# Attention of an adaLN layer: scores from two fp16 parts, the product with V in two halves of queries, and another order of the work around the maxima

## What is computed

```python
h = _layernorm(x, axis=-1) * (1 + ca) + sa
q = (hidden_states @ Wq).reshape(b, s, N_HEADS, HEAD_DIM)      # b, s = 1, 1024; 16 heads of 16
k = (hidden_states @ Wk).reshape(b, s, N_KV_HEADS, HEAD_DIM)   # 4 heads
v = (hidden_states @ Wv).reshape(b, s, N_KV_HEADS, HEAD_DIM)
q = _apply_rope(q, position_ids)
k = _apply_rope(k, position_ids)
scores = jnp.einsum('bshd,bthd->bhst', q, k) * scale
attn = jax.nn.softmax(scores, axis=-1)
out = jnp.einsum('bhst,bthd->bshd', attn, v)
return out.reshape(b, s, HIDDEN) @ Wo
```

## Time and profile before

| | before |
|---|---|
| median of 3 runs | 431.61 us (431.3 to 431.68) |
| the profiled execution, first to last instruction | 458.5 us |
| PE busy | 423.1 us, 92% |
| DVE busy | 318.8 us, 70% |
| ACT busy | 247.3 us, 54% |
| POOL busy | 152.9 us, 33% |
| granted TensorE clock, mean | 0.978 |

### The profile page before, as it was taken

How to read it: one execution, slowest core, us unless ns; L and a number is a source line. 1 busy time by engine, 2 the same in 40 slices (tenths; PEclk the granted TensorE clock), 3 DMA queues, 4 the chain that set the end, 5 groups by cost and what they waited for, 6 DMA issues and landing times.

```text
span 458.5 us, 9187 instructions
## 1 busy us (share of the span) xinstructions
PE 423.1 (92%) x3449; PEld 224.7 (49%) x3449; DVE 318.8 (70%) x739; ACT 247.3 (54%) x406; POOL 152.9 (33%) x177
## 2 busy tenths in 40 slices
PE   8999899999999999999999998987879878979995
PEld 4555323333333333333577776654545545646673
DVE  6878998999999999943476995464544343345457
ACT  1566678788878888887735254333123223233062
POOL 3068201220303030301210008565655764655400
PEclk9999999999999999999999999989979988999998
DMA  8500000000000000000110762488977886896192
GB/s 270 214 4 2 1 1 2 0 2 1 0 1 1 1 1 2 1 1 0 47 36 12 244 245 67 155 283 297 305 258 257 272 299 206 285 286 227 39 375 76
DMA packets 20535, 54.81 MB, mean 120 GB/s; under 512 B 4513, under 2 KB 8825, under 8 KB 20491
## 3 DMA queue, kind: packets, MB, share of 16 engines
q1 hardware_dynamic: 16075, 45.81, 29.5%
q0 software_dynamic: 4416, 8.41, 5.4%
HBM read 49.74 MB, written 8.13 MB: 126 GB/s over the span
## 4 chain that ended last, share of the span: by engine, by line
PE 63%; DVE 12%; another core or an unknown queue 8%; issue 7%; ACT 4%; DMA 4%; POOL 1%; SPq 0%; POOLq 0%; DVEq 0%; ACTq 0%
PE PM L1379 13%; PE EP L1628 7%; PE EP L1366 6%; PE M L1332 6%; PE EP L1369 6%; PE PM L1332 3%; PE EP L1481 3%; PE PM L1650 2%; PE PM L1661 2%; PE EP L1287 2%; DMA w<-ychoice 1%; ACT w L750 1%; PE EP L1303 1%; DMA wide<-in_wmod 1%
## 5 line engine op out<-in xcount | busy, mean ns | idle before, releaser
L670 ACT ACTIVATE QS<-EP 128x1024 f32<-128x1024 f32 x128 | 124.1, 1022 | 24.9 <-PE EP L1369 24.4
L853 DVE TENSOR_REDUCE mx<-M 128x1 f32<-128x512 f32 x171 | 111.6, 684 | 7.2 <-PE M L1332 4.2
L1628 PE MATMUL EP<-w,QS 128*128 128x352 f32 (+1 forms) x244 | 69.9, 497 | 0.0
L1379 PE MATMUL PM<-QS,VA 128*32 128x512 f32 x512 | 68.2, 605 | 0.0
L723 ACT ACTIVATE OT<-EP 128x176 f32<-128x176 f32 x46 | 14.7, 319 | 95.4 <-PE EP L1628 80.6
L853 DVE TENSOR_REDUCE mx<-PM 128x1 f32<-128x512 f32 x85 | 58.1, 684 | 3.8 <-PE M L1332 3.6
L1332 PE MATMUL M<-KT,QT 64*128 64x512 bf16 x171 | 51.4, 384 | 0.2 <-ACT QTB L625 0.2
L1366 PE MATMUL EP<-QT,KT 64*128 64x512 bf16 x256 | 49.0, 377 | 1.0 <-ACT QT L585 0.5
L1369 PE MATMUL EP<-QTB,xh 34*128 34x512 bf16 x256 | 48.9, 377 | 0.0
L525 POOL DMA_INDIRECT QS<-h2rows,tab x26 | 28.6, 1099 | 44.9 <-DVE tab L1073 37.2
L1481 PE MATMUL EP<-segu,QSB 128*128 128x352 f32 x128 | 41.0, 463 | 0.3 <-issue 0.2
(11 more groups left out here) (288 smaller groups left out, 607.3 us busy)
## 6 DMA issues: line engine op xcount, KB each, us to landing
w<-in_w SPq DMA_DIRECT2D x61, 544.0 KB
w<-ychoice SPq DMA_DIRECT2D x8, 512.0 KB, 7.4
segu<-in_segu SPq DMA_DIRECT2D x1, 1408.0 KB, 10.0
x<-in_x SPq DMA_DIRECT2D x2, 512.0 KB, 4.9
wide<-in_wmod SPq DMA_DIRECT2D x1, 1024.0 KB, 7.4
h2rows<-qkv SPq DMA_DIRECT2D x2, 512.0 KB, 2.9
out<-x SPq DMA_DIRECT2D x8, 128.0 KB, 2.3
sedn<-in_sedn SPq DMA_DIRECT2D x1, 640.0 KB, 10.9
```

The source lines that it names most:

```text
L670: nc.scalar.activation(PT[n % 3][:, 2 * p:2 * p + 2, :], EP[p][:, :, :], ACT.Exp, scale=HD ** -0.5).then_inc(e_done, 1)
L853: nc.vector.tensor_reduce(out=mx[:, u % 2, q, j, c:c + 1], in_=src, axis=AX.X, op=ALU.max).then_inc(m_free, 1)
L1379: ins = mm(PV[HP * j:HP * j + HP, :], VA[:, tt, g, :], PT[n % 3][:, j, :], start=tt == 0, stop=tt == NT - 1)
L1628: ins = mm(BANK[b][lo:lo + n, 0:I13], XGT[b][:, c * P + lo:c * P + lo + n], w[:, r, c * I13:(c + 1) * I13], start=c == 0, stop=c == NC - 1)
```

## The change

- **Scores.** q and k are scaled by powers of two (found from a bound on their size) and written as two fp16 parts, high and low. `QR` holds for each head high, low, high and two columns for the maximum; `KR` holds high, high, low and a constant 2^14. The whole score with the maximum is one product over 50 rows, so `scores(n, p)` has two matmuls in place of four. `KTB` and four of the sixteen items of `QK` are gone.
- **Scale.** New on the way to the first tile: ACT squares the weights (`w_sq`) and the modulation (`mod_rep`), PE multiplies them (four matmuls into BANK[6]), DVE makes the scales (`scales`, `s_scale`), and ACT applies them as it copies each projected tile out, in two instructions with a scale operand. `exp` takes its scale from an operand too. The ones in `VA` become the scale of V.
- **Product with V.** `output(n, half)` makes 256 of the 512 queries. The tiles for the maxima stand between the parts of a step.
- **The first maximum.** The transposition of the first two items stands ahead of the projection of tiles 6 and 7, tile 7 behind the first two tiles for the maxima. `QK_COUNT` is later in most places.
- **Maxima to q.** POOL's `minus_max` has three instructions in place of two; `transpose_B` stands behind all tiles of its step.

The core of the diff:

```diff
@@
-        half = 2 * (n + LEAD < STEPS)
-        fills += half
+        fills += 4 * (n + LEAD < STEPS)
+        if n % NT == NT - 2 and n < STEPS - 2:
+            fills += 1
+            Q_FILL.append(fills)
         if n % NT == 1 and n > NT:
             fills += 1
             O_FILL.append(fills)
...
-        QK = [(0, "K", 0, 0), (0, "Q", 0, 0), (0, "Q", 0, 2), (0, "K", 0, 2), (0, "Q", 0, 4), (0, "Q", 0, 6),
-              (1, "K", 0, 0), (1, "K", 0, 2), (0, "K", 1, 0), (0, "K", 1, 2), (1, "K", 1, 0), (1, "K", 1, 2),
-              (1, "Q", 0, 0), (1, "Q", 0, 2), (1, "Q", 0, 4), (1, "Q", 0, 6)]
-
-        QK_COUNT, MOD_AT = (6, 6, 8, 8, 10, 12, 13, 15, 16, 16), (1, 1, 2, 3, 4, 4, 5, 6)
+        QK = [(0, "K", 0), (0, "Q", 0), (0, "Q", 2), (0, "K", 2), (1, "K", 0), (0, "Q", 4), (0, "Q", 6), (1, "K", 2),
+              (1, "Q", 0), (1, "Q", 2), (1, "Q", 4), (1, "Q", 6)]
+
+        QK_COUNT, MOD_AT = (2, 3, 4, 5, 6, 7, 8, 10, 12, 12), (1, 1, 2, 3, 4, 4, 5, 6)
...
+                pool.tensor_tensor(part_m[:, u % 2], negm[:, u % 2], down[:, :, :], ALU.mult).then_inc(s_part, 1)
+                pool.wait_ge(s_part, u + 1)
+                pool.tensor_copy(part[:, :, :, MR_ROWS], part_m[:, u % 2]).then_inc(s_negh, 1)
...
             turn_half_1(0, NH).then_inc(s_ropes, 1)
-            parts_of_k_in_B(0)
+            pool.wait_ge(s_split, 4)
+            repeat_q(0)
             pool.wait_ge(s_qs, 1)
-            pool.tensor_tensor(q1, q1, q_part(HALVES[1], 0), ALU.subtract).then_inc(s_qs, 1)
...
+            pool.tensor_tensor(q_part(HALVES[1], 1), q1, q_part(HALVES[1], 0), ALU.subtract).then_inc(s_qs, 1)
+            repeat_q(1)
...
+            act.wait_ge(ld_qkv, 16)
+            nc.scalar.activation(w_sq, wqkv[:, :, 0:(NH + NG) * HD], ACT.Square)
+            act.wait_ge(s_const, 1)
             act.wait_ge(s_modc, 1)
+            for k in range(2):
+                for c in range(NC):
+                    ins = nc.scalar.activation(mod_rep[:, k, c, :], ones[:, :], ACT.Square, scale=modc[:, k, c:c + 1])
+            ins.then_inc(s_sq, 1)
...
-                nc.scalar.activation(qkv[:, t, :], BANK[(7 + t) % 8][:, 0:QKV], ACT.Copy).then_inc(s_qkvev, 1)
+                if t == 0:
+                    act.wait_ge(s_scale, 1)
+                for i, cols in enumerate((slice(0, NH * HD), slice(NH * HD, QKV))):
+                    ins = nc.scalar.activation(qkv[:, t, cols], BANK[(7 + t) % 8][:, cols], ACT.Copy, scale=powf[:, i:i + 1])
+                ins.then_inc(s_qkvev, 1)
...
-            for n in range(2, 6):
+            for n in range(2, 8):
+                if n == 4:
+                    later_mod(0)
                 qk(n)
-            qk(6)
-            qk(7)
             act.wait_ge(s_ropes, 1)
             nc.scalar.activation(q_part(HALVES[1], 0), q1, ACT.Copy).then_inc(s_qs, 1)
...
-                    nc.scalar.activation(PT[n % 3][:, 2 * p:2 * p + 2, :], EP[p][:, :, :], ACT.Exp, scale=HD ** -0.5).then_inc(e_done, 1)
+                    nc.scalar.activation(PT[n % 3][:, 2 * p:2 * p + 2, :], EP[p][:, :, :], ACT.Exp, scale=exp_scale[:, 0:1]).then_inc(e_done, 1)
...
                 for i in range(2):
-                    rows = slice(AR * i, AR * i + AR)
-                    mm(EP[p][:, i, :], KT[rows, g, keys], QT[rows, 2 * g + p, queries], start=True, stop=False)
-                for i in range(2):
-                    rows = slice(AR * i, AR * i + BR)
-                    ins = mm(EP[p][:, i, :], KTB[rows, g, keys], QTB[rows, u % 2, p, :], start=False, stop=True)
+                    rows = slice(AR * i, AR * i + SR)
+                    ins = mm(EP[p][:, i, :], KT[rows, g, keys], QTB[rows, u % 2, p, :], start=True, stop=True)
                 ins.then_inc(e_fill, 1)
...
-                    ins = mm(PV[HP * j:HP * j + HP, :], VA[:, tt, g, :], PT[n % 3][:, j, :], start=tt == 0, stop=tt == NT - 1)
-                ins.then_inc(pv_step, 1)
+                    ins = mm(PV[HP * j:HP * j + HP, cols], VA[:, tt, g, :], PT[n % 3][:, j, cols], start=tt == 0 and half == 0,
+                             stop=tt == NT - 1, skip_group_check=True)
+                if half == 1:
+                    ins.then_inc(pv_step, 1)
...
                     scores(n, 0)
-                    scores(n, 1)
                 if k < STEPS:
                     scores_for_max(k, (2, 3))
                 if n:
-                    output(n - 1)
+                    scores(n, 1)
+                    output(n - 1, 0)
+                if k < STEPS:
+                    scores_for_max(k, (0, 1))
+                if n % NT == NT - 2 and n < STEPS - 2:
+                    transpose_B(u + 1)
+                if n:
+                    output(n - 1, 1)
                 if n % NT == 1 and n > NT:
                     transpose_output(u - 1)
-                if n % NT == NT - 2 and n < STEPS - 2:
-                    transpose_B(u + 1)
-                if k < STEPS:
-                    scores_for_max(k, (0, 1))
```

241 lines of the change are left out of this document (122 added, 119 removed).

## The result

The changed kernel is slower: 437.33 us (median of 4 runs, 433.69 to 439.17) against 431.64 of the kernel before on the same chip (4 runs, 431.3 to 431.72). The ratio is 1.0115, 95% interval 1.0088 to 1.0143. The loss of 1.2% is small but clear of the spread. The forecast was 426.8, with 420 to 433 as its range, so it missed both the size and the sign.

A forecast was written before the change was run, and what follows sets the result against it. PE was taken to bound the loop, DVE close behind. First tile at 26.2, DVE's tile work and waits put the last maximum at 192.4, 3.8 us earlier; the last steps win 1.0: 4.8 less, 431.61 to 426.8, range 420 to 433.

The forecast's parts named there:

- the ten steps ahead: From the first tile for the maxima to the loop: DVE waits sum to 5.7 us, 3.5 more than before.
- 2.6 for k = 7: Ahead of the loop, PE's item 8 waits for `s_qs`: DVE idles 2.6 us, bounds 1.5 and 3.
- a clock that leaves 1.00 before 200 us: Sign that the prediction is wrong: PE's granted clock leaving full speed before 200 us.
- Rival 2: PE's clock falls in the wait of k = 7, losing 1 to 3 us of the gain: 428.5 to 430.6; chance 0.14.
- The last steps: Ten steps behind the last maximum, 26.4 us before: net 1.0 us less.
- the unit: Eight steps of the loop: 20.3 us in place of 21.32, 6.8 us less over 54 steps.
- The two stalls: DVE's idle times in each unit: 0.67 us behind `transpose_B`, 0.24 behind `transpose_output`, together 0.9 where 1.9 was lost.
- PE is the bound by 0.09 a step: Loop of the kernel before: PE's step 2.49 us, with a wait of some 0.1, against DVE's 2.40.
- rival 1: DVE goes at its floor, waits of k = 7 and behind `transpose_B` smaller: 419 to 424; chance 0.17.
- Rival 3: Nothing measurable: first-stretch waits of 8 us and 1.3 for the transpositions, 430.8 to 432.4; chance 0.08.
- Rival 4: Slower: each half product costs nearly the whole, losing from 0.82 us a half; about 450 at 1.0; chance 0.08.
- Rival 5: Slower: the clock falls again and again in the loop; about 438 with one fall in each unit; chance 0.08.

The follow-up runs named there:

- e3: Changed kernel with both edits, the high part of q made earlier (e1) and more useless matmuls (e2): 429.43 us, ratio 0.9927 to the kernel before.
- e4: Changed kernel with the product with V whole again, in the new order: 450.93 us, ratio 1.0426 to the kernel before.
- e10: Changed kernel run again unaltered: 436.65 us, ratio 1.012 to the kernel before.
- e1: Changed kernel with ACT making the high part of q (rows 512 and up) ahead of item 5: 433.03 us, ratio 1.0028 to the kernel before.
- e2: Changed kernel with three more useless matmuls at the end of each of k = 2, 3, 6 and 7: 434.2 us, ratio 1.0048 to the kernel before.
- e5: e3 with the old order inside a step and the product whole, fp16 scores kept: 464.47 us on a slower chip, ratio 1.0061 to the kernel before.
- e6: e3 with five useless matmuls in step 0: 457.08 us on a slower chip, ratio 0.9904 to the kernel before.
- e8: e6 with a (wrong) constant as the scale of exp, single execution, usable up to the last exp: last eight exps 7.52 us against 8.15.
- e11: e6 with the second half product ahead of the second two tiles in steps with transpose_B: 427.29 us, ratio 0.9895 to the kernel before.
- e12: e11 with more useless matmuls in k = 9, ahead of the first scores and in step 0: 427.15 us, ratio 0.9895 to the kernel before.
- e9: Kernel before with the product in halves, the second behind the second two tiles: 456.55 us, ratio 1.056 to the kernel before.

## Why the prediction was wrong, point by point

**The step that failed** is "the ten steps ahead": a sum of 5.7 us of waits, worked out at full clock. The changed trace has 11.5 (35.54 from the first reduction to the first exp, less the prediction's 24.0). With 3.5 us more waits and a start 0.2 earlier the first exp belongs at about 56.0; it came at 61.63. At full clock the sum is nearly right: e3, with the clock at 1.00 and no wait in k = 7, has 3.3 (27.32 less 24.0), and the prediction without its 2.6 for k = 7 has 3.1. What it put at nothing in the main case is the clock: 1.2 GHz from 38 to 58 us, some 5.3 us of the 35.54 (35.54 less 27.32 less the wait of 2.91). Its own sign of being wrong, a clock that leaves 1.00 before 200 us, came true. The prediction had moved the items to later steps and counted what each adds to DVE's waits, but had not asked what that leaves on PE. It left waits of 0.54 and 0.80 and a window in which PE was busy for 1.20 of 2.00; before, PE was drawn busy for all of every such window from 28 to 44 us.

**What sets off a fall** is not settled. In three of the four profiles with these two waits (the changed kernel, e4, e10) the clock fell within 3 us behind the second; in e1 it did not. In the seven profiles with more useless matmuls there (e2, e3, e5, e6, e8, e11, e12), where the waits are gone or down to 0.20, it never fell at that place. The falls in the first steps go the same way: six of the seven profiles without useless matmuls in step 0 have one (the changed kernel, e1, e2, e3, e5, e10; not e4), one of the four with them (e8). All runs agree: mean clocks are 0.967 to 0.983 for the changed kernel, 0.985 to 0.996 for e3, 0.997 and more for e12, against 0.987 and more for the kernel before on that chip. So that more work on PE keeps the clock is shown as a tendency. That it is the waits is argued: no experiment was made with the waits alone, and the kernel before has a window with PE busy for 1.13 of 2.00 (50 to 52 us) and no fall behind it. The Trainium skill tells of a clock that swings because of short idle times between groups of matmuls ("TensorE: Matmul & The Clock Gate", "A second HAM failure mode: psum-queue depth-cycling"); three of the four traces with such waits agree up to 72 us, e1 does not, and in the loop of e4 PE waits for 0.35 in each step while the clock stays at 1.00.

**Rival 2** had the mechanism and a chance of 0.14: a fall in the wait of k = 7. e2 shows it. Its price, 1 to 3 us, fits e2: against e3 the stretch from the first reduction to the first exp is 4.1 longer, of which 2.96 is the wait and 1.1 the clock. In the changed kernel the clock had fallen 12 us before PE's part of that wait, and a second fall, at 65, took 2.4 more in the first eight steps (20.56 us; 18.13 before and 18.17 in e6, both without a fall); for neither was there a term.

**Right, with small errors:** the first tile (26.09 for 26.2, within a scatter of 1.4 us, so in part luck); the wait of k = 7 and its chain (2.91 for 2.6); the plain step at DVE's floor (2.39 for 2.40); the exp 0.092 longer (1.114 against 1.022) for 0.11, hidden in the loop by e8. The Trainium skill's 93 ns for a pointer operand ("ScalarE: Activation LUTs", "What ACT_TABLE_LOAD costs") is what the trace gives, closer than the 0.12 of the neighbouring rows. The last steps won 1.3 for 1.0; counted from step 55 they also hold the end of what the prediction had in its loop.

**Mis-sized: the unit,** 20.62 for 20.3. The gain is 0.70 in each of five units, not 1.0, and only 0.18 in the last of the six of the table (22.17 for 22.35), which holds projections: 3.7 us in all. The two stalls are larger than worked out. An idle time is drawn 0.08 shorter than the delay of the next start, so 0.70 and 0.38 are delays of 0.78 (103.00 less 102.22) and 0.46; the prediction had 0.67 and 0.24, and the difference of 0.33 is that of the unit. For `transpose_output` the rule of the loop says why. A gap may be 2.40 - 1.48 = 0.92 and the plain one is 0.57 + 0.22 = 0.79, so 0.13 is to spare and not 0.26: the half was taken as 0.53, and the way from a tile to the work behind it as 0.22 where it is 0.31. `transpose_output` takes 0.59 (109.41 to 110.00) and not 0.50. So 0.46 is left.

**Wrong in its reason, right in its result: what bounded the loop.** "PE is the bound by 0.09 a step" took the 2.49 as PE's work with a wait of 0.1. It was the loop through DVE's release and the whole product. In e5 PE lost 0.44 of work and the step stayed at 2.48. So the two parts of the change need each other and the order: in place of 21.32 a unit is 24.73 with halves and the second beside the scores (e9), 22.89 with the new order and the product whole (e4), and 21.67 with light scores in the old order (e5).

**Rivals 1, 3, 4 and 5.** DVE has two stalls in each unit, so rival 1 did not happen. Rival 3 had 8 us of waits in the first stretch; there are 11.5, by the clock, which it did not name. Rival 4 is out by the 0.57 of a half, but e9 shows a way to its loss that it did not name. Rival 5, falls in the loop, did not happen: no profile has one between 82 us and the last exp.
